# A cross-attention block on one core: a prologue of its own, with loads in order of need

## What is computed

```
x   = layer_norm(hidden, ln1_w, ln1_b)
q   = x @ q_w + q_b ;  k = ctx @ k_w + k_b ;  v = ctx @ v_w + v_b      (16 heads of 32)
s   = q @ k.T / sqrt(32), masked ;  out = softmax(s) @ v
hid = out @ cproj_w + cproj_b + hidden
y   = gelu(layer_norm(hid, ln2_w, ln2_b) @ fc_w + fc_b) @ proj_w + proj_b
return hid + y
```

## Time and profile before

| | |
|---|---|
| median of 3 runs | 764.95 us (764.66 to 768.26) |
| profiled execution | 765.3 us, span 763.5 us |
| mean granted TensorE clock | 0.963 |
| TensorE busy | 703.7 us, 92% |
| VectorE, ScalarE, GpSimd busy | 60%, 42%, 33% |

### The profile page before, as it was taken

How to read it: one execution, slowest core, us unless ns; L and a number is a source line. 1 busy time by engine, 2 the same in 40 slices (tenths; PEclk the granted TensorE clock), 3 DMA queues, 4 the chain that set the end, 5 groups by cost and what they waited for, 6 DMA issues and landing times.

```text
span 763.5 us, 13145 instructions
## 1 busy us (share of the span) xinstructions
PE 703.7 (92%) x4544; PEld 610.1 (80%) x4544; DVE 460.8 (60%) x860; ACT 322.2 (42%) x581; POOL 251.0 (33%) x217
## 2 busy tenths in 40 slices
PE   4489989899998989999889999999999999999998
PEld 3378879798888889888667888888888888888886
DVE  5367978988788897978877766442325223151213
ACT  4237766867676686757652121112211121211110
POOL 3505656655545665655752212000000001000000
PEclk9788989999999999999889999999999999999999
DMA  9756554644455464434604500010001000010001
GB/s 247 203 139 176 160 159 123 166 138 154 139 153 153 124 168 111 135 103 143 180 30 125 165 1 1 0 56 1 2 0 56 0 0 0 0 55 1 1 0 57
DMA packets 51130, 69.16 MB, mean 91 GB/s; under 512 B 8328, under 2 KB 29192, under 8 KB 51088
## 3 DMA queue, kind: packets, MB, share of 16 engines
q1 hardware_dynamic: 50816, 68.07, 30.8%
q0 software_dynamic: 272, 0.54, 0.4%
HBM read 47.21 MB, written 20.99 MB: 89 GB/s over the span
## 4 chain that ended last, share of the span: by engine, by line
PE 68%; issue 10%; POOL 6%; DVE 5%; DMA 4%; SPq 3%; ACT 3%; DVEq 0%; ACTq 0%; POOLq 0%
PE psum L1172 8%; PE psum L1174 8%; PE psum L1173 8%; PE psum L1159 7%; PE psum L1157 7%; PE psum L1158 7%; PE psum L975 5%; PE psum L977 5%; PE psum L976 5%; POOL p_lo L462 5%; PE psum L1009 2%; DMA stacks<-qk_rows 2%; PE psum L1059 2%; DMA qk_rows<-qk 2%; PE psum L993 1%
## 5 line engine op out<-in xcount | busy, mean ns | idle before, releaser
L462 POOL TENSOR_TENSOR p_lo<-p,p_hi 128x512 f16<-128x512 f32 x128 | 156.0, 1228 | 137.6 <-ACT p_hi L535 137.3
L662 ACT ACTIVATE h<-psum,cols 128x512 f32<-128x512 f32 x64 | 44.1, 690 | 290.0 <-PE psum L1159 290.0
L913 DVE CAST h_hi<-h 128x512 fp32r<-128x512 f32 x64 | 27.6, 432 | 207.3 <-ACT h L662 207.3
L533 ACT ACTIVATE p<-psum,maskbias 128x512 f32<-128x512 f32 x128 | 88.3, 690 | 47.2 <-PE psum L993 46.1
L1172 PE MATMUL psum<-w_mlp,h_hi 128*128 128x512 f32 x256 | 100.7, 393 | 0.9 <-DVE hidden L758 0.9
L1174 PE MATMUL psum<-w_mlp,h_lo 128*128 128x512 f32 x256 | 99.7, 390 | 0.0
L1173 PE MATMUL psum<-w_mlp,h_hi 128*128 128x512 f32 x256 | 99.7, 390 | 0.0
L1157 PE MATMUL psum<-y_hi,w_mlp 128*128 128x512 f32 x256 | 99.7, 389 | 0.0
L1159 PE MATMUL psum<-y_hi,w_mlp 128*128 128x512 f32 x256 | 99.7, 389 | 0.0
L1158 PE MATMUL psum<-y_lo,w_mlp 128*128 128x512 f32 x256 | 99.6, 389 | 0.0
L535 ACT ACTIVATE p_hi<-psum,maskbias 128x512 f16<-128x512 f32 x128 | 88.8, 694 | 0.0
(11 more groups left out here) (104 smaller groups left out, 1514.2 us busy)
## 6 DMA issues: line engine op xcount, KB each, us to landing
qk_rows<-qk SPq DMA_DIRECT2D x32, 512.0 KB, 2.7
stacks<-qk_rows SPq DMA_DIRECT2D x64, 256.0 KB
stacks<-qk_rows SPq DMA_DIRECT2D x64, 128.0 KB
hidden<-in_x_dram SPq DMA_DIRECT2D x8, 512.0 KB, 4.4
ctx_sb<-in_ctx_dram SPq DMA_DIRECT2D x8, 512.0 KB, 5.3
w_mlp_raw<-in_L_xattn_fc_w_dram SPq DMA_DIRECT2D x16, 256.0 KB, 4.5
w_mlp_raw<-in_L_xattn_proj_w_dram SPq DMA_DIRECT2D x16, 256.0 KB, 6.2
out_dram<-hidden SPq DMA_DIRECT2D x16, 256.0 KB, 2.1
```

Source lines behind the costliest of these rows:

```text
L462: pool.tensor_tensor(p_lo[:, slot, :], p32[:, u % 2, :], p_hi[:, slot, :], ALU.subtract).then_inc(s["p_lo_done"], 1)
L533: act.activation(p32[:, u % 2, :], psum[:, ST + kc, :], ACT.Exp, bias=maskbias[:, kc:kc + 1], scale=SCALE32)
```

## The change

The steps (-2, 2), (-2, 3) and (-1, 0) are replaced by a written-out `first` for each engine. TensorE transposes ctx(0) into banks 2 and 3, which the values use later, ahead of x(0). Group 0 projects k before q, each with its own wait. SP's order becomes x(0), mask, ctx(0), first pieces (k, then q), ln1 columns, v in two halves, bias columns, piece 1, the mask row's store with no wait behind it, piece 2. x(1), piece 3 and the mask as columns are issued after group 0's copies (step (-1, 1)); ctx(1) and the c weight after group 1's (step (-1, 2)). The wait for the mask row's landing stands ahead of its first copy. ScalarE splits pieces 2 and 3 in the steps (-1, 2) and (-1, 3), where it also splits c and fills the mask bias; VectorE does the low parts there. GpSimd makes v's low part in two halves, and c's in step (-1, 3). In step (-1, 2) TensorE does the second v product ahead of the scores. The helper `normed_x` holds the normalisation that stood in VectorE's step, and `statistics` the wait for x; `context_hi` and `context_lo` read `ctx_bank` instead of `in_bank`, and `iterations` is called with `first` on the other engines as well.

```diff
@@ -196,7 +197,7 @@
                     return None
                 return ("qk_lo_done", (G + 1) * 2) if kind == "qk" else ("mrow_ready", G + 1)
             b = it + {"v": 1, "att": -1, "c": -1 - n, "x": 2, "ctx": 1}[kind]
-            if not batch(b):
+            if not batch(b) or (kind == "ctx" and isinstance(b, int) and b == 0):
                 return None
             return {"v": ("v_added", b * 2 + (n + 1)), "att": ("att_lo_done", b * 2 + (n + 1)),
                     "c": ("hidden_added", b * 2 + (n + 1)), "x": (("x_affine_act", "x_affine_dve")[n], b * 2 + 2),
...
+        def ctx_bank(it, j):
+
+            return psum[:, PV + j, :] if isinstance(it, int) and it == -1 else in_bank("ctx", j)
+
...
-        def iterations(eng, step, first_weights=None, weights=None, tail=None):
-
-
-
-
-            for g in range(2, NG):
-                step(-2, g)
-            if first_weights:
-                first_weights()
-            step(-1, 0)
-            if weights:
-                weights()
+        def iterations(eng, step, first=None, tail=None):
+
+            if first:
+                first()
             for g in range(1, NG):
                 step(-1, g)
...
             def load_qk_piece(c):
 
-                for n, w in ((0, q_w), (1, k_w)):
+                for n, w in ((1, k_w), (0, q_w)):
                     sp.dma_start(w_att_raw[:, n, 1, :, c * P:(c + 1) * P],
-                                 w[:, c * P:(c + 1) * P].rearrange("(k p) n -> p k n", p=P)).then_inc(wqk_loaded[c], 16)
+                                 w[:, c * P:(c + 1) * P].rearrange("(k p) n -> p k n", p=P)).then_inc(
+                                     s["wk0_loaded"] if (c, n) == (0, 1) else wqk_loaded[c], 16)
 
             load_x(0)
+            load_small(mrow_raw[:, :], mask, "maskrow_loaded")
+            load_ctx(0)
+            load_qk_piece(0)
             load_small(cols[:, LN1W:LN1W + KT], column(ln1_w), "ln1_loaded")
             load_small(cols[:, LN1B:LN1B + KT], column(ln1_b), "ln1_loaded")
-            load_ctx(0)
-            load_qk_piece(0)
-            load_small(mrow_raw[:, :], mask, "maskrow_loaded")
+            for h in range(2):
+                sp.dma_start(w_att_raw[:, 2, 1, 2 * h:2 * h + 2, :],
+                             v_w[2 * h * P:(2 * h + 2) * P].rearrange("(k p) n -> p k n", p=P)).then_inc(wv_loaded[h], 16)
             load_small(cols[:, QB:QB + KT], column(q_b), "qkb_loaded")
             load_small(cols[:, KB_:KB_ + KT], column(k_b), "qkb_loaded")
-            sp.dma_start(w_att_raw[:, 2, 1, :, :], v_w.rearrange("(k p) n -> p k n", p=P)).then_inc(s["wv_loaded"], 16)
-            for c in range(1, NG):
-                load_qk_piece(c)
-            load_small(maskcol_raw[:, :], mask.rearrange("b (c p) -> p (b c)", p=P), "maskcol_loaded")
-            sp.dma_start(w_att_raw[:, 3, 1, :, :], c_w.rearrange("(k p) n -> p k n", p=P)).then_inc(s["wc_loaded"], 16)
-            load_x(1)
+            load_qk_piece(1)
             sp.wait_ge(s["mask_ready"], 1)
             sp.wait_ge(s["pool_consts"], 5)
             sp.dma_start(mask_rows, maskrow[:, :, :]).then_inc(s["mask_stored"], 16)
-            sp.wait_ge(s["mask_stored"], 16)
+            load_qk_piece(2)
 
...
             def step(it, g):
                 G = it * NG + g + 3
                 b = it if g == 0 else it + 1
                 if g == 0 and batch(it + 2) and not (isinstance(it, int) and it == -1):
                     load_x(it + 2)
-                if g == 1 and batch(it + 2):
+                if g == 1 and batch(it + 2) and not (isinstance(it, int) and it == -1):
                     load_ctx(it + 2)
...
                     slot = slice(GH * ((g + 3) % NG), GH * ((g + 3) % NG) + GH)
+                    if isinstance(G, int) and G == 0:
+                        sp.wait_ge(s["mask_stored"], 16)
...
+                if isinstance(it, int) and (it, g) == (-1, 1):
+                    load_x(1)
+                    load_qk_piece(3)
+                    load_small(maskcol_raw[:, :], mask.rearrange("b (c p) -> p (b c)", p=P), "maskcol_loaded")
+                if isinstance(it, int) and (it, g) == (-1, 2):
+                    load_ctx(1)
+                    sp.dma_start(w_att_raw[:, 3, 1, :, :], c_w.rearrange("(k p) n -> p k n", p=P)).then_inc(s["wc_loaded"], 16)
...
-            def constants():
+            def first():
+                inverse_std(0, TT, "ln_var", "ln_rstd")
                 small(vb_bc[:, :], repeated(v_b), "small_loaded")
                 small(cb_bc[:, :], repeated(c_b), "small_loaded")
-                split_weight_lo(3)
+                for h in range(2):
+                    pool.wait_ge(s["w_hi_act"], h + 1)
+                    cut = slice(2 * h, 2 * h + 2)
+                    pool.tensor_tensor(w_att[:, 2, 1, cut, :], w_att_raw[:, 2, 1, cut, :], w_att[:, 2, 0, cut, :].bitcast(fp32),
+                                       ALU.subtract).then_inc(s["w_lo_v"], 1)
...
-            def split_weight_lo(n):
-
-                pool.wait_ge(s["w_hi_act"], n - 1)
-                pool.tensor_tensor(w_att[:, n, 1, :, :], w_att_raw[:, n, 1, :, :], w_att[:, n, 0, :, :].bitcast(fp32),
+            def split_c_weight():
+
+                pool.wait_ge(s["w_hi_act"], 3)
+                pool.tensor_tensor(w_att[:, 3, 1, :, :], w_att_raw[:, 3, 1, :, :], w_att[:, 3, 0, :, :].bitcast(fp32),
                                    ALU.subtract).then_inc(s["w_lo_pool"], 1)
...
+                if isinstance(it, int) and (it, g) == (-1, 3):
+                    split_c_weight()
...
             def qk_weights_hi(c):
-                act.wait_ge(wqk_loaded[c], 32)
-                for n in range(2):
...
+                for n in (1, 0):
+                    if c == 0:
+                        act.wait_ge(s["wk0_loaded"] if n == 1 else wqk_loaded[0], 16)
+                    else:
+                        act.wait_ge(wqk_loaded[c], 32)
                     act.activation(w_att[:, n, 0, :, c * P:(c + 1) * P], w_att_raw[:, n, 1, :, c * P:(c + 1) * P],
                                    ACT.Copy).then_inc(s["w_hi_qk"], 1)
...
+            def v_weights_hi(h):
+                act.wait_ge(wv_loaded[h], 16)
+                act.activation(w_att[:, 2, 0, 2 * h:2 * h + 2, :], w_att_raw[:, 2, 1, 2 * h:2 * h + 2, :],
+                               ACT.Copy).then_inc(s["w_hi_act"], 1)
+
+            def c_weights_hi():
+                act.wait_ge(s["wc_loaded"], 16)
+                act.activation(w_att[:, 3, 0, :, :], w_att_raw[:, 3, 1, :, :], ACT.Copy).then_inc(s["w_hi_act"], 1)
+
+            def first():
+                context_hi(-1, 0)
+                context_hi(-1, 1)
+                qk_weights_hi(0)
+                affine_x(0)
+                v_weights_hi(0)
+                x_hi(0)
+                v_weights_hi(1)
+                qk_weights_hi(1)
                 act.wait_ge(s["qkb_loaded"], 32)
...
                 qk_high(it, g)
-                if isinstance(it, int) and (it, g) == (-1, 1):
-                    weights_hi(3, "wc_loaded")
-                    act.wait_ge(s["mask_ready"], 3)
-                    mask_columns(0)
-                if isinstance(it, int) and (it, g) == (-1, 0):
-                    x_hi(0)
+                if isinstance(it, int) and it == -1 and g >= 2:
+                    qk_weights_hi(g)
...
-                if g == 3 and batch(it + 1) and not (isinstance(it, int) and it == -1):
+                if isinstance(it, int) and (it, g) == (-1, 3):
+                    c_weights_hi()
+                    act.wait_ge(s["mask_ready"], 3)
+                if g == 3 and batch(it + 1):
                     mask_columns(it + 1)
...
-            def qk_weights_lo(c):
-                for n in range(2):
-                    dve.wait_ge(s["w_hi_qk"], 2 * c + n + 1)
+            def qk_weights_lo(c, which=(1, 0)):
+                for n in which:
+                    dve.wait_ge(s["w_hi_qk"], 2 * c + 2 - n)
...
-            def first_weights_lo():
-                qk_weights_lo(0)
+            def first():
+                statistics(0, [t for t in range(TT)], "ln_stats", "ln_mv", "ln_var")
                 dve.wait_ge(s["maskrow_loaded"], 16)
 
                 dve.tensor_scalar(maskrow[:, 1, :], mrow_raw[:, :], MASKED, -MASKED, ALU.mult, ALU.add).then_inc(s["mask_ready"], 1)
 
-            def weights_lo():
-                dve.wait_ge(s["w_hi_act"], 1)
-                dve.tensor_tensor(w_att[:, 2, 1, :, :], w_att_raw[:, 2, 1, :, :], w_att[:, 2, 0, :, :].bitcast(fp32),
-                                  ALU.subtract).then_inc(s["w_lo_v"], 1)
-                for c in range(1, NG):
-                    qk_weights_lo(c)
+                normed_x(0)
+                context_lo(-1, 0)
+                context_lo(-1, 1)
+                qk_weights_lo(0, (1,))
+                affine_x(0)
+                qk_weights_lo(0, (0,))
+                x_lo(0)
+                qk_weights_lo(1)
...
@@ -817,21 +852,16 @@
```

(70 more changed lines are left out.)

11 lines of the change are left out of this document (1 added, 10 removed).

## The result

The changed kernel takes 762.02 us (median of 20 runs, 757.79 to 768.75), the kernel before 766.4 beside it (20 runs, 763.32 to 772.68): ratio 0.9958, 95% interval 0.9938 to 0.9978, some 3.2 us (the medians are 4.4 apart). Two more measurements gave 0.9966 [0.9943, 0.9989] and 0.9921 [0.989, 0.9951]. So it is faster by a little, in the first measurement by about half of the 7.0 us forecast. The profiled execution took 761.63 us.

What follows compares the result with a forecast made beforehand. Bound at the start by the order of one DMA queue, not arithmetic: group 2 6.2 us earlier plus 0.8 overlap gives 7.0, kept through the loop; 765.3 - 7.0 = 758.3, at the median 757.9; range 753.5 to 762.5.

Steps and rivals of the forecast that it cites:

- Loads before the mask store: SP's queue at the start: 3072 KB ahead instead of 5632, no mask wait before group 0's store, piece 1 in at 16.1.
- Group 0's store at 19.0: Start: group 0's qk store issued at 19.0 (17.5 to 20.3) instead of 26.78, first scores possible at 28.0, 10.3 earlier.
- v's low split goes from VectorE (2.3 us) to GpSimd: Start: GpSimd takes 2.3 us a half, 12.2 to 16.8, done before v's first product, which waits until 19 anyway.
- What stands between the groups: SP's queue: deferred loads delay later stores; group 1's copies at 33.7, 6.1 earlier, group 2's at 45.2, 6.2 earlier.
- 0.8 us of overlap: SP's queue: one group's copies and the next's store overlap, worth 0 to 2 us, taken as 0.8, making 7.0 earlier.
- v's second product ahead of the scores: TensorE, step (-1, 2): fills time before copies arrive; may hold scores up to 3 us, for which group 2's round trip has room.
- c weight and mask columns: Step (-1, 3): ScalarE ready for exponentials at 47.3, 8.7 earlier; GpSimd's 4.59 us split delays p about 1.7, hidden by its buffers.
- The sum: End of the start: TensorE's group 2 scores at 50.7 instead of 57.69, 7.0 us earlier.
- Nothing in the loop changes: Attention loop: same instructions at 43.6 us an iteration, so the 7.0 us shift of its start is kept to the end.
- rival (e): Loop: start shifts but the end does not, as something not begun earlier paces the loop: 764.5 us, chance 0.06.
- rival (b): SP's queue is slower than priced, so group 2 comes only 3 us earlier: 762 us, chance 0.12.
- c in ScalarE's queue: Step (-1, 3): ScalarE stands still until c lands, first exponential 4.5 us later if c lands at 57: 769.4 us, chance 0.04.

Runs made afterwards that it cites:

- both edits: The changed kernel with c's low part left out but for two columns and v's low halves on VectorE instead of GpSimd: 760.72 us, 0.9931 of the kernel before.
- v alone: The changed kernel with v's low halves on VectorE, GpSimd waiting for them: 763.01 us, 0.9949 of the kernel before.
- c in pieces: The changed kernel with v's low halves on VectorE and GpSimd's c split in four pieces, one per step of iteration 0: 755.66 us, 0.9896.
- c after the start: As c in pieces, but c loaded after step (0, 2), its high part in (0, 3), low pieces in (1, 0) and (1, 1): 759.01 us, 0.9942.
- v's second product behind: As c after the start, but v's second product comes after group 0's first scores, as before the change: 757.55 us, 0.9895.
- the eight instructions: The changed kernel with v's low halves on GpSimd in eight instructions instead of two: one execution, 761.62 us.
- the columns behind: The changed kernel with GpSimd's three column loads issued only after piece 1's low parts: one execution, 763.25 us.
- The two versions with both put right: The changed kernel with v low on VectorE, column loads later, c after the start; v's second product after or ahead of group 0's scores: 759.92 (0.9894), 759.14 us (0.9892).

## Why the prediction fell short, step by step

**Loads before the mask store.** Right: SP no longer waits for the mask row's landing ahead of group 0's store, and piece 1's high parts began at 16.22 where 16.1 was forecast (17.55 and 16.61 in the two further profiles). In the first profile v's load in two DMAs ahead of it did not make piece 1 late.

**Group 0's store at 19.0: the step that failed.** "v's low split goes from VectorE (2.3 us) to GpSimd" was priced only as to who needs its result, and at nothing for VectorE; "VectorE's piece 1 low halves (1.28)" were to add 0.3. In fact VectorE's subtracts, which read two operands from SBUF, wait for GpSimd's running instruction: x low takes 2.56 instead of 1.23 in every profile of the change, piece 1's pair 2.74 to 4.06 instead of 1.29. What x low loses does not reach the store, for VectorE then stands idle for 0.72 to 2.65 us until piece 1's high parts come. What the pair loses does: from its start to the store 3.6 to 4.9 us pass, 4.4 on the mean, and 2.2 with v's low part back on VectorE. The store goes at 20.87 to 23.14, 21.8 on the mean, so 2.8 late, 2.2 of it by the pair and 0.6 because the high parts themselves came later in these executions. With v's low part back on VectorE it goes at 18.94, 19.12 and 19.14 (both edits; v alone; c in pieces).

GpSimd's v split is not all of it. In each of the change's three profiles one of the pair ran beside GpSimd's column issues alone and took 1.59 or 1.75; in the version with c after the start the one beside the issues took 1.79, and so did the one beside the bias add; with the issues moved behind, the second of the pair took 0.68. But in four profiles (v alone, both edits, c in pieces, v's second product behind) both ran beside the first two issues, wholly or in part, at 0.68 or 0.69 each. So an issue can hold VectorE and need not; what decides stays open.

Which instructions are held, the traces say in part. x low, whose inputs are both in SBUF, takes 2.56 beside the split, 1.61 beside quarter-size instructions and 1.23 beside none. VectorE's instructions with one input in PSUM were not held: beside the c split of the two further profiles of the change, of v alone, of the eight instructions and of the columns behind, group 3's qk low parts took 0.87 or 0.88 for the two and ctx's first low part 0.68, as without a split. What else decides is not shown.

**What stands between the groups.** The mechanism held, the size was too small: with the store at 18.94 the copies of group 1 still came at 34.35 (33.7 forecast) and those of group 2 at 46.64 (44.5 to 45.2), scores at 52.30 instead of 50.7. The 0.8 us of overlap that I took off was not there, and from group 1's copies to group 2's it took 12.3 instead of the 11.5 that the rows gave without it. Behind ctx and c the store needed 7.0 us, without c 3.3.

**v's second product ahead of the scores.** It held them somewhat longer than "up to 3 us": group 0's scores came at 34.98 where the copies, issued at 25.22, would by their 6.25 us have let them start at 31.5, group 1's low parts being late and v's first product running at the low clock (granted 0.50, 0.43 us for 512 columns; its second one, at 1.00, took 0.23). That this costs nothing later was forecast, and the times with either order, 759.92 and 759.14 us, show no cost; but in both, most of that product ran at the low clock, with marks at 53.12 and 52.90, and the execution that had it at 1.00, v's product behind, has its mark at 50.78. What the order costs at a granted clock of 1.00 is open.

**c weight and mask columns.** The 4.59 us split is "hidden" in TensorE's sense and for p, as forecast. That it can hold VectorE's 128x8 cast for 4.50 us was missed; it did so in one profile of six, and leaving the split out gave no gain to be told.

**The sum.** Group 2's scores, which were to come about 7 us earlier, came 1.7 earlier in the profile (56.00). Marks, as means of three profiles each: before 59.43, the change 57.15, with v's low part back on VectorE 54.14 (v alone, both, c in pieces). So of 7.0 us forecast for the start 2.3 came, 3.0 came back with v's low part on VectorE (0.6 of them, as said, because piece 1 was in earlier), and 1.7 is left, which fits the 1.6 by which group 2's scores are late without that hold (52.30 for 50.7, both edits). How much of the 3.0 reaches the end is not shown. The three measurements of the change average 0.9948, the seven of versions with v's low part on VectorE 0.9914, 2.6 us less; but these seven carry other edits too, and three of them ran on a chip on which the change was not measured. The four that ran beside it are shorter by 0.4, 2.7, 0.6 and 1.4 us by the medians.

**"Nothing in the loop changes", so a shift is kept.** True of the work, too simple for the time. The earlier trace rows already had iterations of 43.6 us at granted clock 1.00 and 44.2 at 0.96, so they were not "all alike", as rival (e) was answered. How many of the second kind come differs from execution to execution, and the time with it: the change itself ran from 757.79 to 768.75, a spread of three times its gain. From the mark to the end the span took 700.4 to 705.3 us in three profiles of before, 701.5 to 701.9 in three of the change, and 699.9 to 706.4 in the three with v's low part on VectorE: as much as all that the start could win. Held back by 6.7, the kernel before lost 4.6 (2.2 to 6.9): a shift is kept to between 0.3 and all. How far exactly, and what decides which iterations run at the lower clock, stays open; so the 3.2 us of the first measurement can't be split into start and loop.

**Chances and rivals.** The prediction drew its line for "faster" at 761.1, 0.5% below; 762.02 is above it, and 0.9958 is 0.4%. So the direction was right, but by its own line the outcome is the "same", which had 0.11, and not the "faster" with 0.85. It is still in the range, near its upper end (762.5), just where rival (b), a slower queue, stood; the kernel before was 1.45 us longer here than the 764.95 that the forecast started from. But its mechanism made up a third of the start's loss only (1.7 of 4.7); the larger part was no rival of mine. That the figure fell on (b)'s is luck. That c in ScalarE's queue makes it slower fell: the first exponential is at 51.94.

## What to carry to other kernels

Moving v's low part from VectorE to GpSimd was not free for VectorE, even where nothing waited for the result: x low took 2.56 us instead of 1.23, piece 1's pair 2.74 to 4.06 instead of 1.29. So before such a move look at which VectorE instructions run in the same window (those held here had all their inputs in SBUF), add up to one GpSimd instruction to each (here 1.3 us beside one of 2.4 for x low, 4.3 beside one of 4.57 for the cast), and ask which of these VectorE would have stood idle behind anyway. A small instruction whose duration is a multiple of its usual one, without idle time ahead of it, as the cast's 4.50 for 0.17, is the sign in a profile. And a load deferred past one store was paid again where it stood in the same queue ahead of the next: group 2's store took 7.0 us behind ctx and c and 3.3 without c, so 3.7 for the 1024 KB; defer it beyond the last of them. The two versions with both put right took 0.989 of the time before, 7.6 and 8.4 us less by the medians (767.51 before); but the change itself was 7.0 us less in that measurement, so what the repairs add is 0.6 and 1.4 us. An edit of 1 to 3 us at the start of a kernel whose executions spread over 11 us is read from its timeline first, and its time only against a neighbour on the same chip.

## What the runs showed of the hardware beyond expectation

- GpSimd is held too: for as many elements as its c split took 4.59 for the earlier trace rows, the two halves of v took 5.70 beside VectorE's subtracts.
- While GpSimd only issues small column loads, 0.75 to 1.16 us each, a VectorE tensor_tensor of 0.68 can take 1.59 to 1.79 (five times, in five profiles), and need not (0.68 or 0.69 for each of the pair in four profiles).
- A cast of 128x8 can take 4.50 us instead of 0.17.
- Iterations of the same instructions take 42.7 to 43.1 us at granted clock 1.00 and 44.2 at 0.96 within one execution of the change; three in a row ran at 0.96 in the first profile of before and with v's second product behind, at 1.00 in the first further profile of the change and with c in pieces.
